# Two subtractions of the dense front move from VectorE to GpSimd, under a new merge table

## The chip, the cores and the metric

The kernel runs on one core of a Trainium2 chip. The metric is the time of one execution on the device in microseconds; lower is better. The engines of a core are TensorE (matmuls and transposes; its weight loads have a lane of their own in the profile), VectorE, ScalarE and GpSimd. Each works through its own list of instructions in order; SyncE only issues transfers here. Engines wait for each other through semaphores.

## What is computed

Two layers over x of 4 x 2048 tokens with 256 channels, all in float32. Each layer has two halves, and each half works on a layer norm of x that is scaled and shifted by rows from a conditioning vector:

```python
h = layernorm(x) * (1 + ca) + sa          # layer 0
x = x + ga * mamba(h)                     # selective scan, 512 inner channels, 16 states
h = layernorm(x) * (1 + cb) + sb
x = x + gb * dense(h)                     # router probability times one expert, gelu, 256 -> 1024 -> 256
h = layernorm(x) * (1 + ca) + sa          # layer 1
x = x + ga * delta_attn(h)                # linear scan over tokens, projection, layer norm
h = layernorm(x) * (1 + cb) + sb
x = x + gb * mixture(h)                   # gated attention-like block, then 2 relu^2 experts and a third
```

## The kernel before

The 8192 tokens are cut into 16 chunks of 512 (NCH), four to a batch row. Channels lie on the 128 partitions in two halves (KC = 2), so one tile of a chunk's 256 channels is 2 x (128 x 512).

Products that have to be exact are made from split operands: a high part (the value copied to the fp32r type) and a low part (value minus high part), multiplied as high x high, high x low, low x high (`split3`, six matmuls for 256 input channels). So each such input needs a copy on ScalarE and two subtractions, one for each half of the channels. For the dense half the input is `ff1`, its high part `f1h` and its low part `f1l`; `ff1` and `f1l` share memory.

Three streams run at once:

- the s stream, layer 0's scan, in 99 steps a chunk: mean, norm, mean, norm, turn, bc (local steps 0 to 5), dt 0 to 3 (6 to 9), gates and ct (10 to 14), z (15 to 18), softplus (19 to 22), 68 units (23 to 90), and a tail of 8 steps. In unit k VectorE does one scan of 512 tokens (line 1195) on the product `dA` that ScalarE makes into PSUM (line 1009) and on `bu` that GpSimd makes (line 909); TensorE turns the states (`hT`), and VectorE sums them into `acc` (line 1153).
- the f stream, the dense half of the chunk before: statistics (a_stats), `rstd_a`, a_norm (gives `nF`), TensorE turns it (`h1T`), ScalarE scales it to `ff1` (line 1023) and copies it to `f1h` (line 1029), the low parts, router, c0 to c7 (up products and gelu), d0 to d7 (down products), x2.
- the x stream, layer 1 of the chunk before that: norms e, h, i, j, m (`rstd_*` is a power of -0.5 that GpSimd takes, line 902; VectorE waits for it in the second half of the norm), x_bias and h_bias (GpSimd adds a row to a 128 x 1024 tile, lines 953 and 958), kq, scan, ao, lowx (`fl`), r, v, sW, and the experts o and p.

How the three are merged on each engine is written down in the table `PACE`: for every piece of the f and x streams the step of the s stream before which it is issued. Step numbers count on over chunks: 105 for chunk j is local step 6 (dt 0) of chunk j + 1, 204 is local step 6 of chunk j + 2. `weave` walks the s steps; before each it issues the pieces that are due, those of the f stream first. On an engine the order is all that the numbers set: a piece does not start at a time, it stands in a queue, behind all that was issued before it.

The pieces around the change: in the front GpSimd has its s steps mean 0, mean 1 and norm 1 (two 128 x 1024 operations, lines 921 and 922) and then none up to softplus 0. TensorE's PSUM banks go round: dt 0 takes the bank that gate 0 needs again, and it is freed by ScalarE's exponential of dt 0 (line 983). VectorE subtracts `xnl` (line 1180) before TensorE can do bc. The table places act's `h1T` and `h1h` at 105, before its dt 0.

Of the kernel before, what the change touches and what calls it, by code (L numbers as in the profile page):

```python
# [6 lines left out]
F32 = mybir.dt.float32  # L7
F32R = mybir.dt.float32r
ALU = mybir.AluOpType
# [9 lines left out]
KC = C // P  # L19
# [126 lines left out]
def since(eng, sig, chunk, k=0):  # L146

    if sig.at(chunk, k) > 0:
# [3 lines left out]

PACE = {
    "sp": {
        "mod_f": 57, "ffn_0": 83, "ffn_1": 87, "ffn_0_down": 98, "ffn_1_down": 108, "mod_x": 191, "rv": 230,
        "sw": 237, "e0_0": 238, "e0_1": 255, "e0_0_down": 258, "e0_1_down": 258, "e1_0": 266, "e1_0_down": 269,
        "e1_1": 273, "e1_1_down": 273, "out": 289,
    },
    "pool": {
        "rstd_a": 103, "rstd_e": 186, "x_bias": 186, "h_bias": 191, "rstd_h": 202, "rstd_i": 202, "rstd_j": 205,  # L160
        "rstd_m": 252,
    },
    "act": {
# [6 lines left out]
    },  # L170
    "dve": {
        "a_stats": 100, "a_norm": 104, "low0": 105, "low1": 108, "router": 110, "prob": 124, "ffn0": 152,
        "ffn1": 153, "scaled": 153, "x2": 153, "e_stats": 191, "e_norm": 191, "kq0": 198, "kq1": 198, "kq2":
        199, "kq3": 199, "beta": 199, "scan0": 201, "qs0": 202, "scan1": 202, "qs1": 202, "ao0": 203, "ao1":
        203, "h_stats": 203, "h_norm": 203, "i_stats": 204, "i_norm": 206, "j_stats": 206, "j_norm": 208,
        "lowx0": 208, "lowx1": 208, "v0": 234, "v1": 238, "att0": 245, "att1": 247, "m_stats": 248, "m_norm":
        249, "lowh0": 251, "lowh1": 251, "bids": 256, "tw0": 257, "tw1": 257, "choice": 257, "tr": 258, "e0":
        274, "e1": 291, "x5": 291,
    },
# [12 lines left out]
    },  # L192
}

# [1 line left out]
def build(nc, w, out):  # L196
    ctx = ExitStack()
    with ctx:
# [22 lines left out]
        def signal(name, n):  # L221
            return Signal(sem(name), n)
# [42 lines left out]
        f1h = sb("f1h", [P, KC, CT], F32R)  # L265
        f1l = sb("f1l", [P, KC, CT], F32R)
        ff1 = over("ff1", [P, KC, CT], "f1l")
# [46 lines left out]
        prob = sb("prob", [P, NT])  # L314
        sm = sb("sm", [P, NT, 3 * NH])
        bl = sb("bl", [P, NT, 8])
        sg = sb("sg", [P, NT, 4])
# [75 lines left out]
        f_fh = signal("f_fh", KC)  # L393
        f_fl = signal("f_fl", KC)
# [391 lines left out]
        with nc.Block() as block:  # L786
# [113 lines left out]
            def _(pool):  # L900
                def rstd(rs, sig):
                    pool.tensor_tensor(rs[:, :], rs[:, :], mhalf[:, :], ALU.pow).then_inc(sig.sem, 1)  # L902
# [35 lines left out]
                def f_stream(j):  # L938
                    yield "rstd_a"
                    pool.wait_ge(f_mv.sem, f_mv.at(j, 1))  # L940
                    rstd(rs_f, f_rs)

                def x_stream(j):
                    def norm(k):
# [166 lines left out]
            def _(dve):  # L1111
# [107 lines left out]
                def f_stream(j):  # L1219
# [7 lines left out]
                    since(dve, f_x2, j)  # L1227
                    dve.wait_ge(f_rs.sem, f_rs.at(j, 1))
                    apply(nF, x1, mv_f, rs_f, f_n)
                    for c in range(KC):  # L1230
                        yield f"low{c}"
                        dve.wait_ge(f_fh.sem, f_fh.at(j, c + 1))
                        dve.tensor_tensor(f1l[:, c, :], ff1[:, c, :], f1h[:, c, :].bitcast(F32), ALU.subtract)\
                           .then_inc(f_fl.sem, 1)
                    yield "router"
                    b = take(dve, j, "routerT")
                    dve.tensor_copy(lg[:, :, :], b.t[:, 0:NT * 8].rearrange("p (t e) -> p t e", t=NT))\
# [444 lines left out]
```

## Time and profile before

| | us |
|---|---|
| median of three runs | 3918.71 (3918.51 to 3923.24) |
| the profiled execution | 3923.29 |
| its span, first to last instruction | 3921.5 |

| engine | busy, us | share of the span | instructions |
|---|---|---|---|
| TensorE matmul | 3080.0 | 79% | 14772 |
| VectorE | 3124.9 | 80% | 5517 |
| ScalarE | 2143.5 | 55% | 3193 |
| GpSimd | 1694.7 | 43% | 1289 |

The mean granted TensorE clock is 0.878 of full speed. Busy shares are averages over stages: a front, where many short pieces wait for each other, and the units, where VectorE scans. They have to be read apart.

### The profile page before, as it was taken

The page shows a single profiled execution, that of the slowest core. Times are in us where ns is not written, and L with a number is a line of the kernel's source. Part 1 is how long each engine was busy: PE and PEld are TensorE (multiplying, and loading weights), DVE is VectorE, ACT ScalarE, POOL GpSimd, SP SyncE. Part 2 cuts the span into 40 slices and gives each one's busy share as a digit, 9 for nine tenths or more (in the row PEclk, how much of TensorE's full clock was granted, in tenths as well). Part 3 has the DMA queues.
Part 4 walks back from the last instruction along what each step waited for, and adds up shares of the span by engine and source line. Part 5 has one row for each costly group of instructions (what it writes and reads, how often), then busy time and mean ns, then how long its engine had stood idle before and what let it go on. Part 6 is the DMA issues. An engine that isn't in the chain of part 4 may idle for free. (4 is left out here: it accounts for less than half of the span.)

```text
span 3921.5 us, 44935 instructions
## 1 busy us (share of the span) xinstructions
PE 3080.0 (79%) x14772; PEld 2484.7 (63%) x14772; DVE 3124.9 (80%) x5517; ACT 2143.5 (55%) x3193; POOL 1694.7 (43%) x1289
## 2 busy tenths in 40 slices
PE   3556688797887879788787878888797978879668
PEld 1445467576675767576676757667576756757556
DVE  5777889797888879898888879798897979888331
ACT  0426375655647475564747466564747556474322
POOL 0535454453535354453545445353545445353000
PEclk7658689898998989898998989899998989989878
DMA  6110113121221312121221312122131212212111
GB/s 221 34 54 25 56 65 108 57 89 59 88 71 61 111 62 84 57 96 63 82 81 65 117 41 95 56 87 82 56 108 62 86 64 84 71 67 95 54 59 70
DMA packets 143008, 298.31 MB, mean 76 GB/s; under 512 B 18084, under 2 KB 87732, under 8 KB 125364
## 3 DMA queue, kind: packets, MB, share of 16 engines
q1 hardware_dynamic: 142232, 292.29, 22.0%
q8 instruction: 119, 1.95, 0.2%
q10 hardware_dynamic: 272, 1.57, 0.1%
q0 software_dynamic: 272, 1.57, 0.1%
q14 instruction: 113, 0.93, 0.1%
HBM read 278.04 MB, written 17.35 MB: 75 GB/s over the span
## 5 line engine op out<-in xcount | busy, mean ns | idle before, releaser
L909 POOL TENSOR_TENSOR bu<-z,bb 128x512 f32<-128x512 f32 x1024 | 1307.4, 1285 | 889.2 <-DVE hs L1195 656.1
L1195 DVE TENSOR_TENSOR_SCAN hs<-ps_A,state,bu 128x512 f32<-128x512 f32 x768 | 977.5, 1275 | 78.3 <-ACT ps_A L1009 61.8
L1009 ACT ACTIVATE ps_A<-dt,a_neg 128x512 f32<-128x512 f32 x1024 | 690.1, 686 | 514.1 <-DVE hs L1195 511.1
L1429 PE MATMUL ps_H<-ident,hs 128*128 128x128 f32 x4096 | 655.4, 299 | 308.8 <-DVE hs L1195 167.0
L1429 PEld LDWEIGHTS ps_H<-ident,hs 128*128 128x128 f32 x4096 | 526.6, 154 | 447.7 <-issue 199.2
L1153 DVE SCALAR_TENSOR_TENSOR acc<-ps_H,ctok,acc 128x512 f32<-128x512 f32 x960 | 697.2, 729 | 68.3 <-PE ps_H L1429 67.8
L1533 PE MATMUL ps_B<-ws_out,hid 128*128 128x256 f32 x3072 | 727.0, 381 | 30.8 <-ACT hid L1040 18.0
L1533 PEld LDWEIGHTS ps_B<-ws_out,hid 128*128 128x128 f32 x3072 | 565.6, 190 | 120.2 <-ACT hid L1040 24.3
L1434 PE MATMUL ps_B<-fh,ws_in 128*128 128x512 f32 x1536 | 599.2, 434 | 14.9 <-DMA ws_in<-w_split 4.8
L902 POOL TENSOR_TENSOR rs_x<-rs_x,mhalf 128x4 f32<-128x4 f32 x80 | 90.7, 1134 | 770.5 <-DVE rs_x L1120 770.5
L1434 PEld LDWEIGHTS ps_B<-fh,ws_in 128*128 128x128 f32 x1536 | 305.0, 199 | 78.8 <-DMA ws_in<-w_split 5.2
L1195 DVE TENSOR_TENSOR_SCAN hs<-ps_A,bu 128x512 f32<-128x512 f32 x256 | 310.5, 1215 | 42.5 <-ACT ps_A L1009 34.1
L1434 PE MATMUL ps_B<-f1h,ws_in 128*128 128x512 f32 x512 | 235.0, 510 | 119.1 <-ACT hid L1040 58.0
L1434 PE MATMUL ps_B<-fl,ws_in 128*128 128x512 f32 x768 | 313.5, 408 | 0.0
L1104 ACT ACTIVATE hid<-ps_B 128x512 f32<-128x512 f32 x256 | 150.5, 588 | 256.9 <-PE ps_B L1434 254.7
L1009 ACT ACT_TABLE_LOAD x191 | 245.1, 1283 | 3.4
L1434 PEld LDWEIGHTS ps_B<-f1h,ws_in 128*128 128x128 f32 x512 | 123.7, 242 | 167.5 <-ACT hid L1040 71.7
L1434 PEld LDWEIGHTS ps_B<-fl,ws_in 128*128 128x128 f32 x768 | 153.7, 200 | 22.0
L1106 ACT ACTIVATE hid<-hid 128x512 f32<-128x512 f32 x256 | 161.6, 631 | 8.2
L1405 DVE SCALAR_TENSOR_TENSOR hA<-ps_B,coef,hA 128x256 f32<-128x256 f32 x192 | 79.5, 476 | 96.1 <-PE ps_B L1533 93.8
L1273 DVE TENSOR_TENSOR fl<-ff,fh 128x512 fp32r<-128x512 f32 x64 | 67.5, 1094 | 105.9 <-ACT fh L1054 105.9
L928 POOL TENSOR_TENSOR z<-z,dt 128x512 f32<-128x512 f32 x64 | 83.8, 1310 | 136.1 <-ACT dt L996 136.1
(265 smaller groups left out, 4617.8 us busy)
## 6 DMA issues: line engine op xcount, KB each, us to landing
ws_in<-w_split SPq DMA_DIRECT2D x128, 1024.0 KB, 4.8
bb<-b_rows SPq DMA_DIRECT2D x256, 256.0 KB, 3.4
ws_out<-in_L_ffn_V_rwkv SPq DMA_DIRECT2D x64, 512.0 KB, 4.9
ws_out<-in_L_ffn_W SPq DMA_DIRECT2D x32, 512.0 KB, 5.3
w_split<-ws_in SPq DMA_DIRECT2D x8, 1024.0 KB, 4.9
xraw<-in_L_attn_x SPq DMA_DIRECT2D x16, 512.0 KB, 4.6
out<-xb SPq DMA_DIRECT2D x16, 512.0 KB, 3.3
stage<-in_L_ffn_K_rwkv SPq DMA_DIRECT2D x4, 512.0 KB, 6.7
```

The source lines that it names most:

```text
L902: pool.tensor_tensor(rs[:, :], rs[:, :], mhalf[:, :], ALU.pow).then_inc(sig.sem, 1)
L909: pool.tensor_tensor(bu[:, u % 4, :], z[:, d, :], bb[:, s % 2, :], ALU.mult).then_inc(s_bu.sem, 1)
L928: pool.tensor_tensor(z[:, k, :], z[:, k, :], dt[:, k, :], ALU.mult).then_inc(s_u.sem, 1)
L1009: act.activation(b.t[:, :], dt[:, d, :], ACT.Exp, scale=a_neg[:, d, s:s + 1])\
L1104: act.activation(hid[:, k, :], b.t[:, :], ACT.Relu).then_inc(b.free, 1)
L1106: act.activation(hid[:, k, :], hid[:, k, :], ACT.Square).then_inc(x_sq.sem, 1)
L1153: ins = dve.scalar_tensor_tensor(out=acc[:, t, :], in0=b.t[:, :], scalar=ctok[:, t, s:s + 1], in1=acc[:, t, :], op0=ALU.mult, op1=ALU.add)
L1195: dve.tensor_tensor_scan(hs[:, s % 2, d, :], b.t[:, :], bu[:, k % 4, :], state[:, s, d:d + 1] if i % CPB else 0.0, ALU.mult, ALU.add)\
L1405: ins = dve.scalar_tensor_tensor(out=hA[:, t, :], in0=b.t[:, t % 2 * C:(t % 2 + 1) * C], scalar=coef[:, t, e:e + 1], in1=hA[:, t, :], op0= ...
L1429: return pe.transpose(dst, src, ident[:, :])
L1434: last = pe.matmul(dst, a, b, start=n == 0, stop=n == len(prods) - 1)
L1533: last = pe.matmul(b.t[:, t % 2 * C:(t % 2 + 1) * C], hid[:, k, t * P:(t + 1) * P], wt[:, k % HB, :], start=k == 0 and t % 2 == 0, stop=k ...
```

## The change

GpSimd makes the low halves of the dense front's input in place of VectorE, with the same operation on the same tiles and the same semaphores. The table `PACE` is made anew for all engines: some 90 numbers move, most by one or two steps. The larger moves, and those that change an order around the front, are in the cut of the diff.

```diff
 PACE = {
     "sp": {
-        "mod_f": 57, "ffn_0": 83, "ffn_1": 87, "ffn_0_down": 98, "ffn_1_down": 108, "mod_x": 191, "rv": 230,
-        "sw": 237, "e0_0": 238, "e0_1": 255, "e0_0_down": 258, "e0_1_down": 258, "e1_0": 266, "e1_0_down": 269,
+        "mod_f": 65, "ffn_0": 90, "ffn_1": 94, "ffn_0_down": 100, "ffn_1_down": 105, "mod_x": 191, "rv": 230,
+        "sw": 242, "e0_0": 243, "e0_1": 260, "e0_0_down": 261, "e0_1_down": 264, "e1_0": 273, "e1_0_down": 273,
...
     "pool": {
-        "rstd_a": 103, "rstd_e": 186, "x_bias": 186, "h_bias": 191, "rstd_h": 202, "rstd_i": 202, "rstd_j": 205,
-        "rstd_m": 252,
+        "rstd_a": 105, "rstd_e": 196, "x_bias": 196, "h_bias": 204, "rstd_h": 215, "rstd_i": 215, "rstd_j": 215,
+        "rstd_m": 252, "low0": 107, "low1": 107,
     },
     "act": {
-        "h1T0": 105, "h1T1": 105, "h1h0": 105, "h1h1": 105, "router": 120, "lexp": 124, "c0": 126, "c1": 126,
+        "h1T0": 105, "h1T1": 105, "h1h0": 105, "h1h1": 105, "router": 120, "lexp": 124, "c0": 125, "c1": 125,
...
-        "q": 195, "kvT0": 196, "kvT1": 196, "xlT0": 218, "xlT1": 218, "xlh0": 218, "xlh1": 218, "r0": 235, "r1":
+        "q": 195, "kvT0": 196, "kvT1": 196, "xlT0": 218, "xlT1": 218, "xlh0": 220, "xlh1": 220, "r0": 235, "r1":
...
     "dve": {
-        "a_stats": 100, "a_norm": 104, "low0": 105, "low1": 108, "router": 110, "prob": 124, "ffn0": 152,
-        "ffn1": 153, "scaled": 153, "x2": 153, "e_stats": 191, "e_norm": 191, "kq0": 198, "kq1": 198, "kq2":
+        "a_stats": 102, "a_norm": 104, "low0": 105, "low1": 105, "router": 111, "prob": 124, "ffn0": 152,
+        "ffn1": 152, "scaled": 152, "x2": 152, "e_stats": 191, "e_norm": 191, "kq0": 198, "kq1": 198, "kq2":
...
-        203, "h_stats": 203, "h_norm": 203, "i_stats": 204, "i_norm": 206, "j_stats": 206, "j_norm": 208,
+        203, "h_stats": 203, "h_norm": 203, "i_stats": 205, "i_norm": 207, "j_stats": 207, "j_norm": 208,
...
     "pe": {
-        "h1T0": 105, "h1T1": 105, "router": 119, "c0": 119, "routerT": 119, "c1": 119, "c2": 120, "c3": 120,
+        "h1T0": 108, "h1T1": 108, "router": 123, "c0": 123, "routerT": 123, "c1": 123, "c2": 123, "c3": 123,
...
@@ -939,6 +939,11 @@
                     yield "rstd_a"
                     pool.wait_ge(f_mv.sem, f_mv.at(j, 1))
                     rstd(rs_f, f_rs)
+                    for c in range(KC):
+                        yield f"low{c}"
+                        pool.wait_ge(f_fh.sem, f_fh.at(j, c + 1))
+                        pool.tensor_tensor(f1l[:, c, :], ff1[:, c, :], f1h[:, c, :].bitcast(F32), ALU.subtract)\
+                            .then_inc(f_fl.sem, 1)
 
@@ -1227,11 +1232,6 @@
                     apply(nF, x1, mv_f, rs_f, f_n)
-                    for c in range(KC):
-                        yield f"low{c}"
-                        dve.wait_ge(f_fh.sem, f_fh.at(j, c + 1))
-                        dve.tensor_tensor(f1l[:, c, :], ff1[:, c, :], f1h[:, c, :].bitcast(F32), ALU.subtract)\
-                           .then_inc(f_fl.sem, 1)
```

## Rows read from the trace of the kernel before

**Rows 1.** Stretches, us: busy of PE, PEld, DVE, ACT, POOL; clock; DMA
```profile
2008.50:2083.30 74.80, 59.99 (x283) 48.54 (x282) 58.52 (x162) 34.58 (x53) 24.86 (x16) 0.87 0.15 50
2083.30:2232.40 149.10, 126.39 (x638) 103.27 (x639) 135.06 (x180) 101.12 (x148) 81.16 (x64) 0.93 0.26 89
2053.30:2075.50 22.20, 22.20 (x106) 17.70 (x104) 18.09 (x61) 14.61 (x22) 3.51 (x3) 1.00 0.15 50
2079.30:2094.20 14.90, 11.63 (x29) 8.15 (x30) 9.56 (x12) 11.67 (x17) 13.81 (x11) 0.50 0.09 32
```

**Rows 2.** Timeline (start, duration in us), TensorE, front of chunk 9
```profile
2053.31 0.58 PE L1434 MATMUL ps_H<-xnh,w_bc_h 128*128 128x512 f32 x1
...
2054.89 1.04 PE L1429 MATMUL ps_B<-ident,nF 128*128 128x128 f32 x8
...
2061.34 0.39 PE L1434 MATMUL ps_H<-w_in_h,xnh 128*128 128x512 f32 x1
...
2073.08 1.03 PE L1429 MATMUL ps_B<-ident,nn 128*128 128x128 f32 x8
...
2079.32 0.77 PE L1434 MATMUL ps_B<-f1h,ws_in 128*128 128x512 f32 x1 [3.82 <-ACT rows_f L1017]
```

**Rows 3.** Timeline, ScalarE, the same front
```profile
2055.58 1.42 ACT L1023 ACTIVATE ff<-ps_B,mod_col 128x512 f32<-128x512 f32 x2
...
2058.06 1.28 ACT L983 ACT_TABLE_LOAD   x1
2059.35 0.69 ACT L983 ACTIVATE dt<-ps_H,bdt_col 128x512 f32<-128x512 f32 x1
...
2075.73 1.43 ACT L1047 ACTIVATE ff<-ps_B,cols 128x512 f32<-128x512 f32 x2
...
2081.53 1.30 ACT L1009 ACTIVATE ps_A<-dt,a_neg 128x512 f32<-128x512 f32 x2
```

**Rows 4.** Timeline, VectorE, the same front
```profile
2051.42 1.29 DVE L1180 TENSOR_TENSOR xnl<-xnf,xnh 128x512 fp32r<-128x512 f32 x2 [2.35 <-ACT xnh L975]
...
2058.95 1.67 DVE L1135 SCALAR_TENSOR_TENSOR xb<-nn,rs_x,xb 128x256 f32<-128x256 f32 x4
...
2070.53 1.38 DVE L1124 TENSOR_SCALAR nn<-hA,mv_x,rs_x 128x256 f32<-128x256 f32 x4
2077.71 3.16 DVE L1273 TENSOR_TENSOR fl<-ff,fh 128x512 fp32r<-128x512 f32 x2 [5.80 <-ACT fh L1054]
2082.78 0.19 DVE L1237 COPY lg<-ps_B 128x32 f32<-128x32 f32 x1 [1.92 <-PE ps_B L1515]
...
2083.34 2.46 DVE L1195 TENSOR_TENSOR_SCAN hs<-ps_A,state,bu 128x512 f32<-128x512 f32 x2
```

**Rows 5.** By source line, whole run: count, ns smallest/median/largest
```profile
L1233 DVE TENSOR_TENSOR f1l<-ff,f1h x32: 681/684/693, 289.0 to 3642.2; 128x512 fp32r<-128x512 f32 x32
...
L909 POOL TENSOR_TENSOR bu<-z,bb x1024: 1258/1278/1612, 125.4 to 3577.0; 128x512 f32<-128x512 f32 x171
```

**Rows 6.** Timeline, GpSimd, front of chunk 9
```profile
2050.31 1.02 POOL L902 TENSOR_TENSOR rs_f<-rs_f,mhalf 128x4 f32<-128x4 f32 x1
2057.42 1.17 POOL L902 TENSOR_TENSOR rs_x<-rs_x,mhalf 128x4 f32<-128x4 f32 x1 [6.09 <-DVE rs_x L1120]
```

**Rows 7.** GpSimd's h_bias by line; timeline of both engines, front of chunk 1
```profile
L958 POOL TENSOR_TENSOR hA<-hA,bo_row x16: 2345/3264/3281, 462.9 to 3779.5; 128x1024 f32<-128x1024 f32 x16
...
279.44 2.34 POOL L922 TENSOR_TENSOR xb<-xraw,h 128x1024 f32<-128x1024 f32 x1
...
280.25 2.68 DVE L1180 TENSOR_TENSOR xnl<-xnf,xnh 128x512 fp32r<-128x512 f32 x2 [3.39 <-ACT xnh L975]
```

**Rows 8.** Timeline of ScalarE, TensorE and VectorE, first units of chunk 9
```profile
2086.17 0.69 ACT L1009 ACTIVATE ps_A<-dt,a_neg 128x512 f32<-128x512 f32 x1 [0.76 <-DVE hs L1195]
...
2088.91 0.79 PE L1434 MATMUL ps_B<-f1h,ws_in 128*128 128x512 f32 x1 [2.96 <-ACT hid L1040]
...
2095.03 0.75 DVE L1150 TENSOR_SCALAR acc<-ps_H,ctok 128x512 f32<-128x512 f32 x1 [2.18 <-PE ps_H L1429]
```

More of the change, by code:

```diff
@@ L154 @@
     "sp": {
-        "mod_f": 57, "ffn_0": 83, "ffn_1": 87, "ffn_0_down": 98, "ffn_1_down": 108, "mod_x": 191, "rv": 230,
-        "sw": 237, "e0_0": 238, "e0_1": 255, "e0_0_down": 258, "e0_1_down": 258, "e1_0": 266, "e1_0_down": 269,
-        "e1_1": 273, "e1_1_down": 273, "out": 289,
+        "mod_f": 65, "ffn_0": 90, "ffn_1": 94, "ffn_0_down": 100, "ffn_1_down": 105, "mod_x": 191, "rv": 230,
+        "sw": 242, "e0_0": 243, "e0_1": 260, "e0_0_down": 261, "e0_1_down": 264, "e1_0": 273, "e1_0_down": 273,
+        "e1_1": 277, "e1_1_down": 277, "out": 293,
     },
     "pool": {
-        "rstd_a": 103, "rstd_e": 186, "x_bias": 186, "h_bias": 191, "rstd_h": 202, "rstd_i": 202, "rstd_j": 205,
-        "rstd_m": 252,
+        "rstd_a": 105, "rstd_e": 196, "x_bias": 196, "h_bias": 204, "rstd_h": 215, "rstd_i": 215, "rstd_j": 215,
+        "rstd_m": 252, "low0": 107, "low1": 107,
     },
     "act": {
[1 row of a table removed]
[1 row of a table added]
         "c2": 129, "c3": 131, "c4": 133, "c5": 138, "c6": 142, "c7": 144, "h2T0": 195, "h2T1": 195, "beta": 195,
[3 rows of a table removed]
[3 rows of a table added]
         275, "p2": 280, "p3": 281, "p4": 284, "p5": 285, "p6": 288, "p7": 288,
```

20 rows, old and new, of the table PACE are left out of this document.

## Prediction

> **What bounds the kernel now.** I read the stretches first. In the middle of the run a chunk takes some 224 us: 74.8 us from the last scan of one chunk to the first scan of the next (tail, then front), and 149 us of units. In the units VectorE is busy 135 of 149 us; in the 75 us it is busy 58.5 us and TensorE 60 us, so neither alone sets them [rows 1]. What happens there is a chain, so I followed one front (chunk 9's, from 2050 us) engine by engine. All times below are of that front.
>
> TensorE issues bc at 2053.31, turns nF at 2054.89, goes through dt, gate and z without a pause and turns nn at 2073.08; the first gate product starts at 2061.34 [rows 2]. ScalarE's copies, logarithms and a table load follow z, then the first exponential for the scans at 2081.53 [rows 3]. VectorE waits 5.8 us for fh, 1.9 us for the router's transposed logits, and scans at 2083.34 [rows 4]. Its two subtractions of f1l lie between h_norm and nn, ahead of these waits, and nn is ready at 2071.9 (2070.53 + 1.38), 1.2 us before TensorE can use it. So the work that is taken off VectorE is not late for anybody. In this front the last to be waited for are TensorE up to z, and then ScalarE.
>
> **The removed work.** Two subtractions of 684 ns, 32 in all, 21.9 us [rows 5]. All of it lies in fronts, where VectorE's own waits [rows 4] swallow it: worth 0 by this chain, and at most 1.4 us a chunk, 22 us in all, if VectorE were last. Moved to GpSimd, each is taken at 1.28 us, the price of the nearest form, its 128x512 product of two SBUF tiles [rows 5]. That is 2.6 us a chunk, in a stretch where GpSimd is idle two thirds of the time [rows 1]. By itself this is harmless. Its place in GpSimd's queue and the new table are not.
>
> **GpSimd's new order.** After its two 1024-wide operations the queue was: rstd_a, then rstd_h as soon as VectorE had the variances [rows 6]. It becomes rstd_a, h_bias (191 to 204), low0 and low1 (107), and only then rstd_h, rstd_i and rstd_j (202 to 215). GpSimd goes in order, so rstd_h waits until ScalarE has made f1h; behind rstd_h stands VectorE's second half of h_norm (2058.95 [rows 4]), and behind that the x3, i and j norms, the clips of dt and nn.
>
> **TensorE's and ScalarE's new order.** TensorE turns nF not right behind bc (105) but after three dt products (108). ScalarE still takes h1T before its first dt exponential (105). So ff1, f1h, a table load and the dt exponentials all slip, and gate 0 needs the bank that the first dt exponential frees.
>
> **h_bias meets xnl.** h_bias takes 2.34 us alone, its smallest time [rows 7]. It moves from the tail to right behind rstd_a, which ends at 2051.33 [rows 6]. VectorE starts xnl at 2051.42 [rows 4]. In the front of chunk 1 the xnl pair began while GpSimd's 1024-wide addition ran (279.44 to 281.78): the pair took 2.68 us for the 1.29 us of chunk 9 [rows 4, 7]. Its first half ended some 0.55 us after GpSimd's operation, as if it had run only then. So I take: h_bias 2051.35 to 2053.7, xnl done at 2054.85 (2053.7 + 0.55 + 0.6) in place of 2052.71. TensorE is ready for bc at 2053.3, so bc starts 1.6 us late. If xnl won the race for its first half, h_bias would get in before the second half and the end would be the same within 0.2 us. The bounds are 0 (h_bias starts too late to matter) and 2.1 us.
>
> The Trainium skill, page "SBUF — State Buffer", section on the shared port pair, speaks against this place: a VectorE operation with two SBUF inputs and a GpSimd operation that reads SBUF exclude each other for a whole instruction, and whoever comes first keeps the ports. By that rule xnl waits for all of h_bias; the row of chunk 1 agrees (2.68 us for 1.29).
>
> **The sum, one front.** bc runs 2054.9 to 2056.5. A product takes 1.40 us: eight of them and the small ct, 0.5 us, lie between 2061.34 and 2073.08 [rows 2]. So three dt products end at 2060.7, the turn of nF at 2061.5, the fourth at 2062.9. ScalarE: ff and f1h, 2.5 us, from 2061.25 to 2063.75, the table load to 2065.0, the first exponential (0.69) to 2065.7 [rows 3]. Gate 0 starts at 2065.75 in place of 2061.34: a stall of 2.85 us. From there to the end of z lie 11.74 us (2073.08 − 2061.34): 2077.5, 4.4 us late.
>
> GpSimd: low0 from 2063.25 (the first f1h), low1 to 2065.8, rstd_h to 2066.9. VectorE waited for it from 2061.1 on. From its restart to the end of nn it now takes 12.95 us (2058.95 to 2071.9); one hidden subtraction less and one clip more exposed make 12.7: nn at 2079.6, 2.1 us after z. TensorE turns nn to 2080.4 and does the router to 2081.8.
>
> ScalarE: z3 at 2077.7, table load, first logarithm to 2080.2; then ff from nn 1.45 us to 2081.65, a logarithm, rows_f to 2082.8, the logarithms and fh (the table places fh two steps later), the table load, and the first exponential to 2087.0, in place of 2082.2. VectorE: fl beside GpSimd's products 84.0 to 86.6, the logits to 87.2, first scan 2087.25. That is 3.9 us later than 2083.34. Bounds: 1.2 us (no collision, TensorE's stall partly covered) and 4.8 us (the exponential's own shift).
>
> **What the units give back.** c0 and c1 move from 126 to 125 on ScalarE, ahead of the fourth exponential. Before, that exponential waited for VectorE until 2086.17 and the two gelus stood behind it; TensorE idled 2.96 us until c2 at 2088.91, then did c2, c3 at half clock and the first hT, for which VectorE waited 2.18 us until 2095.03 [rows 8]. With the gelus at once after the third exponential (85.4), c2 starts 1.4 us earlier. That wait can shrink by 1.4 us; the fourth scan still ends before. ffn0 to x2 move to 152, before the wait for fh of 0.42 us a chunk, and cover it: 0.4. The other moves in the units are of one or two steps, and SyncE's loads stay a few us ahead of their readers; I take 0, bounds ±1 us a front.
>
> **Clock.** In the front TensorE now runs at 1.00; after its 3.8 us pause ahead of c0 it runs at 0.50, the lower of its two levels [rows 1, 2]. The new pause of 2.85 us may bring the same to the gates; there each 1.40 us product would cost 1.2 to 1.4 us more, and I allow for one or two of them. The pause ahead of c0 shrinks from 3.8 to about 1 us and the one ahead of c2 to 1.5, which may give a like amount back. I take +0.3, bounds −2 and +3.4.
>
> Per front: 3.9 − 1.4 − 0.4 + 0.3 = 2.4 us. There are 14 fronts of this kind (chunks 2 to 15): 34 us. Chunk 1's front has no x stream; by the same working, without the exponential's table load, TensorE's stall is 1.9 us, less 1.4: 0.5. Chunk 0 has none. After the last chunk low0 and low1 again stand before rstd_h and cost an estimated 1.0 us (low1's and low0's places against the two subtractions saved); the statistics moved behind kq3, where VectorE waits anyway, give back an estimated 1.4. In all 34 us. The profiled run took 3923.3 us (span 3921.5), the median is 3918.7; I add the 34 to the median: **3953 us**.
>
> **Rivals.**
> 1. *The clock drops in the gates* in most fronts: some two products, 2.5 us, of which nn's lateness hides a little: 14 times about 2.2 = 31 us: 3984. For: the 3.8 us pause was followed by 0.50 [rows 1, 2]. Against: 2.85 us is shorter, and it follows ten busy microseconds. Chance 0.15.
> 2. *h_bias misses xnl and the units give back more*: 1.6 us less and the clock before c2 recovers: 0.5 to 1 us a front: 3926 to 3934. For: the two starts are 0.1 us apart. Chance 0.12, a third of it within 0.2%.
> 3. *VectorE is the bound after all* (other side, faster): if ScalarE's f1h came before VectorE's variances, rstd_h would not be held up, and the front would shrink by VectorE's 1.37 us, the units by 1.8: 15 × 3.2 = 48 us: 3871. The point of decision: low1 must end by 2057.4, when rstd_h starts now; f1h ends at 2058.06, where the table load starts [rows 3], even with the turn in its old place, and now later. Chance 0.08.
> 4. *The change moves nothing that counts*: the front's delay goes into VectorE's idle time at the start of the units (1.9 + 2.2 us). Against: these waits follow from the same chain and move with it. 3915 to 3926, chance 0.07.
>
> The forecast itself (3938 to 3970) has 0.58. Range: from rival 2's low end to just past rival 1: 3926 to 3986, leaving out 3, most of 4 and the far tail. Slower by over 0.2% (7.8 us, about what a measurement of this kernel can tell from no change): 0.58 + 0.15 + 0.08 = 0.81. Within: 0.10. Faster: 0.09.
>
> **What the new profile would show.** If right: GpSimd's rstd_h starts 2.6 us or more after f1h; VectorE's h_norm has a wait of 5 to 7 us released by GpSimd's rs_x, which it did not have; the xnl pair takes about 3.4 us in fronts from chunk 2 on; TensorE pauses 2 to 3 us at the first gate product, released by ScalarE's dt; the units get no longer. Wrong, if xnl stays at 0.69 (no collision), if h_norm doesn't wait, or if the units shrink by more than 3 us. A granted clock under 0.9 between bc and z would speak for rival 1.

## The result, and the profile after

The changed kernel takes 3985.9 us (median, 3983.87 to 3987.83) against 3919.36 us (3918.51 to 3923.24): 1.0168 times as long, interval 1.015 to 1.0185. The prediction said slower, by 34 us; it is slower by 66.5 us. The kernel before was timed again beside each group of experiments, with medians from 3920.6 to 3921.7 us; the ratios given with the experiments are against those. The profiled execution's span is 3984.6 us against 3921.5, so 63.1 of the 66.5 us can be looked for in the traces.

The page of the changed kernel, span and busy times:

```profile
span 3984.6 us, 44935 instructions
...
PE 3100.8 (78%) x14772; PEld 2501.7 (63%) x14772; DVE 3148.7 (79%) x5485; ACT 2144.0 (54%) x3193; POOL 1723.8 (43%) x1321
```

VectorE has 32 instructions fewer and yet 23.8 us more of busy time (3124.9 before): that already says that something holds instructions up while they count as busy. GpSimd has 29.1 us more. TensorE issues the same 14772 matmuls and is busy 20.8 us longer, at a mean granted clock of 0.871 against 0.878.

I then cut both traces at VectorE's scans, into fronts (last scan of a chunk to first scan of the next) and units (first to last scan of a chunk). Sums in us, worked out from the scans' start and end times:

| | prologue | units 0 | front 1 | units 1 | fronts 2 to 15 | units 2 to 15 | drain |
|---|---|---|---|---|---|---|---|
| before | 127.5 | 114.1 | 72.0 | 128.7 | 1076.9 | 2065.9 | 336.5 |
| after | 126.1 | 114.1 | 71.0 | 132.4 | 1149.2 | 2051.6 | 340.2 |
| difference | -1.4 | 0.0 | -1.0 | +3.7 | +72.3 | -14.3 | +3.7 |

A front of chunks 2 to 15 is 5.16 us longer, the units of a chunk 1.02 us shorter. The differences add up to 63.0 us.

The same stretches as in [rows 1], with the same columns, for the changed kernel: the front of chunk 9, its units, and 13.7 us of chunk 7's front, from the first gate product to the end of z:

```profile
2039.90:2119.40 79.50, 59.56 (x286) 47.50 (x285) 60.03 (x161) 34.46 (x53) 26.33 (x18) 0.91 0.14 43
2119.40:2265.90 146.50, 124.44 (x636) 103.33 (x636) 135.67 (x180) 101.19 (x148) 81.36 (x65) 0.93 0.27 93
...
1644.70:1658.40 13.70, 13.56 (x52) 10.18 (x52) 11.44 (x40) 7.42 (x13) 3.21 (x4) 0.88 0.00 1
...
1645.90:1648.90 3.00, 3.00 (x9) 2.18 (x7) 3.00 (x9) 2.38 (x3) 0.00 (x0) 0.50 0.00 0
```

The first two lines: the front grew from 74.8 to 79.5 us with the same work in it, the units went from 149.1 to 146.5. The third: from the first gate product to the end of z TensorE is busy nearly all the time (13.56 of 13.70), but the clock averages 0.88; in the kernel before it was 1.00 in this part. The fourth lies inside the third and shows the granted clock at 0.50 there. I show chunk 7 from here on because chunks 8 and 9 are the two fronts in which the clock held.

TensorE in the front of chunk 7, timeline (start, duration):

```profile
1633.84 0.50 PE L1434 MATMUL ps_H<-xnh,w_bc_h 128*128 128x512 f32 x1
...
1639.54 1.03 PE L1429 MATMUL ps_B<-ident,nF 128*128 128x128 f32 x8
...
1641.57 0.40 PE L1434 MATMUL ps_H<-xnh,w_dt_l 128*128 128x512 f32 x1
1644.72 0.50 PE L1434 MATMUL ps_H<-w_in_h,xnh 128*128 128x512 f32 x1 [2.74 <-ACT dt L988]
...
1646.20 0.63 PE L1434 MATMUL ps_H<-w_in_h,xnl 128*128 128x512 f32 x1
...
1649.94 0.40 PE L1434 MATMUL ps_A<-w_in_l,xnh 128*128 128x512 f32 x1
...
1658.44 1.09 PE L1429 MATMUL ps_B<-ident,nn 128*128 128x128 f32 x8 [0.17 <-DVE nn L1129]
```

The turn of nF now stands behind three dt products, and the first gate product waits 2.74 us for ScalarE's dt. Behind the pause the matmuls go from 0.40 to 0.63 us each and are back at 0.40 by 1649.94. nn is no longer late for TensorE: it waits 0.17 us.

ScalarE, GpSimd and VectorE in the same front, in this order:

```profile
1641.52 1.14 ACT L1034 ACTIVATE f1h<-ff 128x512 fp32r<-128x512 f32 x2
1642.68 1.28 ACT L988 ACT_TABLE_LOAD   x1
1643.98 0.69 ACT L988 ACTIVATE dt<-ps_H,bdt_col 128x512 f32<-128x512 f32 x1
...
1630.29 2.35 POOL L963 TENSOR_TENSOR hA<-hA,bo_row 128x1024 f32<-128x1024 f32 x1
1642.22 2.49 POOL L945 TENSOR_TENSOR f1l<-ff,f1h 128x512 fp32r<-128x512 f32 x2 [9.59 <-ACT f1h L1034]
1644.66 1.02 POOL L902 TENSOR_TENSOR rs_x<-rs_x,mhalf 128x4 f32<-128x4 f32 x1
...
1630.42 3.37 DVE L1185 TENSOR_TENSOR xnl<-xnf,xnh 128x512 fp32r<-128x512 f32 x2 [2.35 <-ACT xnh L980]
1645.82 1.67 DVE L1140 SCALAR_TENSOR_TENSOR xb<-nn,rs_x,xb 128x256 f32<-128x256 f32 x4 [5.83 <-POOL rs_x L902]
1657.00 1.38 DVE L1129 TENSOR_SCALAR nn<-hA,mv_x,rs_x 128x256 f32<-128x256 f32 x4 [0.90 <-POOL rs_x L902]
1664.24 2.89 DVE L1273 TENSOR_TENSOR fl<-ff,fh 128x512 fp32r<-128x512 f32 x2 [5.86 <-ACT fh L1059]
```

All four steps of the prediction are to be seen. The first dt exponential stands behind f1h and a table load and ends when the gate product starts. GpSimd idles 9.59 us for f1h, makes both low halves, and only then rs_x; h_norm waits 5.83 us for it. h_bias (L963) starts 0.13 us ahead of xnl, and the xnl pair takes 3.37 us.

By line, whole run (count, ns smallest/median/largest):

```profile
L945 POOL TENSOR_TENSOR f1l<-ff,f1h x32: 1260/1263/1477, 290.2 to 3689.1; 128x512 fp32r<-128x512 f32 x32
L963 POOL TENSOR_TENSOR hA<-hA,bo_row x16: 2340/2349/2681, 486.3 to 3842.4; 128x1024 f32<-128x1024 f32 x16
L1185 DVE TENSOR_TENSOR xnl<-xnf,xnh x32: 677/1381/2840, 96.5 to 3462.4; 128x512 fp32r<-128x512 f32 x32
```

The moved subtraction costs 1263 ns on GpSimd (684 on VectorE, [rows 5]; 1.28 us was taken). h_bias itself got cheaper (median 3264 ns before, [rows 7]): in its old place it was the one that was held up (in chunk 9 it started while VectorE's line 1215 ran and ended 2.2 us after that). Single xnl halves now reach 2840 ns for a smallest time of 677.

To say what the steps are worth on average, not in one front, I took the same marks in all fronts of chunks 2 to 15, in us after the start of xnl. The copy of z3 is ScalarE's copy of the last z product, the end of the gate and z stretch; h_norm stands for the start of its second half, nn for the start of nn:

| | end of xnl | start of bc | first gate product | copy of z3 | h_norm | nn | first scan |
|---|---|---|---|---|---|---|---|
| before | 1.29 | 2.51 | 10.55 | 22.49 | 7.70 | 19.27 | 32.53 |
| after | 3.39 | 3.44 | 14.30 | 28.03 | 15.40 | 26.59 | 37.99 |
| h1T back (e3) | | | 11.40 | 23.33 | 11.71 | 22.90 | 33.30 |
| pause filled (e9) | | | 14.31 | 26.35 | | | 36.34 |
| rstd_h first (e2) | | | | 28.05 | 9.62 | 23.89 | 38.01 |

From the first gate product to the copy of z3 lie 11.94 us before and 13.73 us after: 1.79 us more for the same products.

### The profile page after: what moved, and what is told of

The parts are those of the page before. It is cut to its first block and busy times, and to the rows that moved or that the text cites. A ratio compares the mean times of both kernels' runs of the same rounds, so it can differ in the third digit from the quotient of the medians.

```text
span 3984.6 us, 44935 instructions
## 1 busy us (share of the span) xinstructions
PE 3100.8 (78%) x14772; PEld 2501.7 (63%) x14772; DVE 3148.7 (79%) x5485; ACT 2144.0 (54%) x3193; POOL 1723.8 (43%) x1321
## 5 line engine op out<-in xcount | busy, mean ns | idle before, releaser
L1434 PE MATMUL ps_B<-f1h,ws_in 128*128 128x512 f32 x512 | 225.1, 496 | 106.5 <-ACT hid L1045 52.5
L1405 DVE SCALAR_TENSOR_TENSOR hA<-ps_B,coef,hA 128x256 f32<-128x256 f32 x192 | 79.5, 475 | 98.2 <-PE ps_B L1533 93.8
L976 ACT ACTIVATE xnf<-ps_A,cols 128x512 f32<-128x512 f32 x32 | 24.9, 777 | 236.3 <-PE ps_A L1429 235.1
L902 POOL TENSOR_TENSOR rs_s<-rs_s,mhalf 128x4 f32<-128x4 f32 x32 | 32.8, 1024 | 264.4 <-DVE rs_s L1125 264.4
```

The lines of the kernel that those rows point to most:

```text
L976: act.activation(xnf[:, c, :], b.t[:, :], ACT.Identity, scale=cols[:, c:c + 1], bias=cols[:, 2 + c:3 + c]).then_inc(b.free, 1)
L1405: ins = dve.scalar_tensor_tensor(out=hA[:, t, :], in0=b.t[:, t % 2 * C:(t % 2 + 1) * C], scalar=coef[:, t, e:e + 1], in1=hA[:, t, :], op0= ...
L1434: last = pe.matmul(dst, a, b, start=n == 0, stop=n == len(prods) - 1)
```

## The experiments

The first theory: the order of the table costs the time, above all h1T's new place, by a chain through ScalarE, and TensorE's clock adds to it. The rivals: the subtraction on GpSimd itself, GpSimd's queue (rstd_h behind the low halves), or h_bias beside xnl.

**The operation alone, and the table alone.** In e5 the kernel before gets the subtractions on GpSimd (the code as in the change) and nothing else:

```diff
-        "rstd_m": 252,
+        "rstd_m": 252, "low0": 105, "low1": 108,
```

> The kernel before with its own table, and only the two subtractions on GpSimd (low0 105, low1 108 there). The prediction's claim: the move itself is worth nothing, since VectorE's part lies ahead of waits and GpSimd is idle: 3915 to 3925. Rival (VectorE is the bound): 1.4 us a chunk less, 3898. Rival (GpSimd is late for rstd_j or the router): 3930 or more.

Measured: 3915.51 us, 0.999 (0.998 to 0.9999), a gain of 5.1 us against the median of 3920.63 in that session. In e6 the changed kernel keeps its table, number for number, and the subtractions go back to VectorE, where the table has low0 and low1 at 105:

```diff
                     rstd(rs_f, f_rs)
-                    for c in range(KC):
-                        yield f"low{c}"
-                        pool.wait_ge(f_fh.sem, f_fh.at(j, c + 1))
-                        pool.tensor_tensor(f1l[:, c, :], ff1[:, c, :], f1h[:, c, :].bitcast(F32), ALU.subtract)\
-                            .then_inc(f_fl.sem, 1)
...
                     apply(nF, x1, mv_f, rs_f, f_n)
+                    for c in range(KC):
+                        yield f"low{c}"
+                        dve.wait_ge(f_fh.sem, f_fh.at(j, c + 1))
+                        dve.tensor_tensor(f1l[:, c, :], ff1[:, c, :], f1h[:, c, :].bitcast(F32), ALU.subtract)\
+                           .then_inc(f_fl.sem, 1)
```

> The changed kernel with the subtractions back on VectorE (105, 105), the new table otherwise. Theory: the late turn of nF costs the same; GpSimd's queue is free of the low parts, which was worth nothing in the run with rstd_h first: 3980 to 3990, as the changed kernel. Rival (the move of the operation is what costs): 3950 or less.

Measured: 3985.09 us, 1.0163 (1.0147 to 1.0178); the first scan comes at 37.97 us, the changed kernel's is at 37.99. The two runs together settle it: the whole loss is in the table. The move of the work costs nothing: under the new table it is worth 0.8 us, which can't be told from 0, and under the old one it brings some 5 us (0.4 to 7.8 by the interval). In e5's trace that gain sits in four of the 14 fronts, where the first scan comes 9.08 us after the copy of z3 in place of some 10.0; the reason is given below, with e11.

**h1T back to 105.** e3 is the changed kernel with one number pair undone on TensorE:

```diff
     "pe": {
-        "h1T0": 108, "h1T1": 108, "router": 123, "c0": 123, "routerT": 123, "c1": 123, "c2": 123, "c3": 123,
+        "h1T0": 105, "h1T1": 105, "router": 123, "c0": 123, "routerT": 123, "c1": 123, "c2": 123, "c3": 123,
```

> The changed kernel with TensorE's turn of nF back at 105, ahead of the dt products. Theory 1: f1h comes 4 us earlier, TensorE has no pause ahead of the first gate product, rstd_h is held up by only 2 to 3 us; what stays is h_bias against xnl, 1.6 us, and a little of nn: 3935 to 3950, about 3940. The clock theory says the same sign and wants the granted clock back at 1.00 between bc and z. Rival (h1T's place is of no weight, GpSimd's queue is): 3975 or more.

Measured: 3914.3 us, 0.9981 (0.9971 to 0.999). That is 71.6 us less than the changed kernel, more than its whole loss, and 26 us less than the 3940 I expected. The expectation priced the pause and not the clock behind it, which e9 puts at 25 us. TensorE in the front of chunk 7:

```profile
1605.46 0.51 PE L1434 MATMUL ps_H<-xnh,w_bc_h 128*128 128x512 f32 x1 [0.91 <-DVE xnl L1185]
...
1606.96 1.04 PE L1429 MATMUL ps_B<-ident,nF 128*128 128x128 f32 x8
...
1613.42 0.40 PE L1434 MATMUL ps_H<-w_in_h,xnh 128*128 128x512 f32 x1
```

nF is turned right behind bc, the first gate product follows without a wait and at 0.40 us, and gate to z3 takes 11.93 us on average, as before (11.94). Per front the first gate product comes 2.90 us earlier, the copy of z3 4.70 us and the first scan 4.69 us. h_norm still waits for GpSimd here and h_bias still meets xnl (bc waits 0.91 us for it), so neither of these can be the main loss.

**Is it the clock?** Of the 4.7 us, the pause explains 2.9. For the other 1.8 the slower matmuls behind the pause are the suspect, but a pause and a clock that falls come together. e9 parts them: it is the changed kernel, and in the pause TensorE does the six matmuls of dt 3 twice more ahead of the real ones (the product is redone with the same result). The gate product can't start earlier by this; only the pause is filled.

```diff
                     if name == "dt":
+                        if k == DB - 1 and i >= 2:
+                            b = fill(pe, i, f"dt{k}")
+                            for _ in range(2):
+                                split3(b.t[:, :], [w_dt["h"][:, c, k * P:(k + 1) * P] for c in range(KC)],
+                                       [w_dt["l"][:, c, k * P:(k + 1) * P] for c in range(KC)],
+                                       [xnh[:, c, :] for c in range(KC)], [xnl[:, c, :] for c in range(KC)])
                         from_xn(i, f"dt{k}", w_dt, k * P)
```

> The changed kernel, with TensorE doing the fourth dt product three times over in chunks 2 to 15 (same result, 24 us... in detail 2 x 1.40 us of extra work a front), so that it works through most of its 2.85 us pause ahead of the first gate product. From gate 0 to ScalarE's copy of z3 the changed kernel takes 13.7 us on average, the kernel before 11.9. Theory (the pause lowers the granted clock): with the pause filled the stretch is 11.9 us again, 1.8 us a front, 25 us in all, against the changed kernel's 3986: about 3961, though 12 more matmuls are done in each front. Rival (the lower clock has another cause, or the work just delays): 3986 to 4010.

Measured: 3960.5 us, 1.0098 (1.0081 to 1.0115): 25.4 us less than the changed kernel, with 2.8 us of matmuls more in every front. TensorE's timeline in chunk 7, its last dt product and its first gate product:

```profile
1631.41 0.40 PE L1434 MATMUL ps_H<-xnh,w_dt_l 128*128 128x512 f32 x1
1631.76 0.50 PE L1434 MATMUL ps_H<-w_in_h,xnh 128*128 128x512 f32 x1
```

and the stretch from there to the end of z (columns as in [rows 1]):

```profile
1631.80:1643.80 12.00, 11.97 (x53) 9.17 (x52) 10.07 (x36) 7.18 (x12) 2.94 (x4) 1.00 0.01 2
```

The first gate product starts at the same place in the front (14.31 us after xnl, 14.30 without the filling), the granted clock is 1.00 where it was 0.88, and the stretch takes 12.0 in place of 13.7 us. The copy of z3 comes 1.68 us earlier, the first scan 1.65 us, and the fronts' sum is 24.9 us smaller (1.78 each). The count over all fronts agrees: with the pause of 2.74 us the granted clock fell behind it in 12 of 14 fronts in the changed kernel, in 14 in e1, 13 in e2 and 12 in e6; without it (e3) or with it filled (e9) in none. So the pause costs twice: by its own length, and by the lower clock that follows it. The filling undoes the second alone.

**GpSimd's queue.** e2 puts rstd_h ahead of the low halves again:

```diff
-        "rstd_a": 105, "rstd_e": 196, "x_bias": 196, "h_bias": 204, "rstd_h": 215, "rstd_i": 215, "rstd_j": 215,
+        "rstd_a": 105, "rstd_e": 196, "x_bias": 196, "h_bias": 204, "rstd_h": 204, "rstd_i": 215, "rstd_j": 215,
```

> The changed kernel with rstd_h at 204, ahead of low0 and low1 in GpSimd's queue; nothing else. Theory 1: VectorE's 5.8 us wait in h_norm goes, but nn was at most 2 us later than z, and in fronts at the lower clock not later at all: 0 to 2 us a front, 5 to 20 us in all, about 3975. Rival (the h_norm wait is the main cost): the 5.8 us come back in each of 14 fronts, 3905 to 3925.

Measured: 3985.48 us, 1.0161 (1.0145 to 1.0176), the same as with the queue; the 5 to 20 us that I expected did not come. The waits of the changed kernel (us in total, times, longest us):

```profile
DVE xb L1140 <- POOL rs_x L902: 81.4, 14, 5.9
...
PEld ps_H L1434 <- ACT dt L988: 46.3, 15, 3.2
```

In e2 the first of these is gone, the second is the same to the digit, and its timeline in chunk 7 has (VectorE, VectorE, TensorE):

```profile
1639.63 1.67 DVE L1140 SCALAR_TENSOR_TENSOR xb<-nn,rs_x,xb 128x256 f32<-128x256 f32 x4
...
1653.89 1.38 DVE L1129 TENSOR_SCALAR nn<-hA,mv_x,rs_x 128x256 f32<-128x256 f32 x4 [0.90 <-POOL rs_x L902]
...
1657.68 1.03 PE L1429 MATMUL ps_B<-ident,nn 128*128 128x128 f32 x8
```

h_norm waits for nothing, nn is ready at 1655.27 (1653.89 + 1.38), and TensorE takes it at 1657.68. 81.4 us of waits, the clearest new wait of VectorE in the whole trace, are worth nothing. With the clock kept (e9) nn really is late:

```profile
1645.56 1.09 PE L1429 MATMUL ps_B<-ident,nn 128*128 128x128 f32 x8 [1.79 <-DVE nn L1129]
...
1644.42 1.28 ACT L1001 ACT_TABLE_LOAD   x1
1645.71 0.63 ACT L1001 ACTIVATE dt<-dt 128x512 f32<-128x512 f32 x1
1646.25 1.45 ACT L1052 ACTIVATE ff<-ps_B,cols 128x512 f32<-128x512 f32 x2
```

TensorE waits 1.79 us, close to the 2.1 us forecast. But ScalarE, for whom the turned nn is meant, is in its table load and first logarithm until then, and takes it without a pause: the lateness hides there too. The marks say the same: from the copy of z3 to the first scan lie 9.99 us in e9 (26.35 to 36.34), and 9.96 in the changed kernel, where nn is hardly late. e9 with rstd_h first wasn't tried.

**h_bias beside xnl.** e1 puts h_bias back into the tail, in the changed kernel; e8 puts it behind rstd_a, in the kernel before. The table rows of e1, and of e8:

```diff
-        "rstd_a": 105, "rstd_e": 196, "x_bias": 196, "h_bias": 204, "rstd_h": 215, "rstd_i": 215, "rstd_j": 215,
+        "rstd_a": 105, "rstd_e": 186, "x_bias": 186, "h_bias": 191, "rstd_h": 215, "rstd_i": 215, "rstd_j": 215,
```

```diff
-        "rstd_a": 103, "rstd_e": 186, "x_bias": 186, "h_bias": 191, "rstd_h": 202, "rstd_i": 202, "rstd_j": 205,
+        "rstd_a": 103, "rstd_e": 186, "x_bias": 186, "h_bias": 204, "rstd_h": 204, "rstd_i": 204, "rstd_j": 205,
```

> The changed kernel with h_bias alone back at 191 (x_bias and rstd_e at 186). Theory 1 (three orders in the front cost the time, each by its own wait): xnl is done 2.1 us earlier, bc starts 1.6 us earlier, and the first scan with it in 14 fronts: 22 us off the changed kernel's 3986, so about 3964. Rival (the clock of TensorE, not the wait, is what costs): the pause ahead of the first gate product stays at 1.5 to 3 us and so does the time, 3980 or more.

> The kernel before with h_bias at 204 (and rstd_h, i, j right behind it): the collision with xnl alone. In the old front bc starts 2.5 us after xnl on average, and would start at 3.44: 0.9 us in 14 fronts, 13 us: about 3933. Rival (the prediction's 1.6 us a front): 3943. Rival (absorbed later in the front): 3921.

Measured: e1 3965.77 us, 1.0111 (1.0096 to 1.0126), 20.1 us less than the changed kernel. e8 3937.32 us, 1.0044 (1.0029 to 1.0059), 16.3 us more than the kernel before in that session (3921.02). xnl by line, of e1 and of e8:

```profile
L1185 DVE TENSOR_TENSOR xnl<-xnf,xnh x32: 679/688/2086, 97.3 to 3441.0; 128x512 fp32r<-128x512 f32 x32
```

```profile
L1180 DVE TENSOR_TENSOR xnl<-xnf,xnh x32: 676/1380/2834, 96.3 to 3423.4; 128x512 fp32r<-128x512 f32 x32
```

One number decides whether the median xnl half takes 688 or 1380 ns. The collision is real and costs in both kernels, but less than its 2.1 us: in e8 the first scan comes 0.78 us later (33.31 against 32.53) in each front, and the units lose 0.58 us a chunk (2074.0 against 2065.9 in all). That second part arises at one place: c2 starts 5.28 us after the first scan (5.29 before), but from there to the first hT lie 5.06 us in place of 4.55, at a mean granted clock of 0.53 in place of 0.60. So some 7 us of e8's loss stand behind slower matmuls; why the clock stays low for longer there was not tried.

**All three back.** e4 puts h1T, h_bias and the whole queue of GpSimd up to rstd_h back, and keeps the rest of the new table and the subtractions on GpSimd:

```diff
-        "rstd_a": 105, "rstd_e": 196, "x_bias": 196, "h_bias": 204, "rstd_h": 215, "rstd_i": 215, "rstd_j": 215,
+        "rstd_a": 103, "rstd_e": 186, "x_bias": 186, "h_bias": 191, "rstd_h": 202, "rstd_i": 215, "rstd_j": 215,
...
-        "h1T0": 108, "h1T1": 108, "router": 123, "c0": 123, "routerT": 123, "c1": 123, "c2": 123, "c3": 123,
+        "h1T0": 105, "h1T1": 105, "router": 123, "c0": 123, "routerT": 123, "c1": 123, "c2": 123, "c3": 123,
```

> The changed kernel with all three orders of before: h_bias 191, rstd_h 202 and h1T at 105; the subtractions stay on GpSimd and the rest of the new table stays. Theory 1: the fronts are as before and the units keep their 1 us of gain each: about 3910, 3900 to 3920. Rival (something else in the new table costs too): 3930 or more.

Measured: 3907.8 us, 0.996 (0.9946 to 0.9974). The first scan comes at 32.40 us, the kernel before has 32.53. So these three moves are the loss, and what is left of the change is a gain of some 14 us against the kernel before in that session (3921.65). Their prices alone (71.6, 20.1 and 0.4 us, from e3, e1 and e2 against the changed kernel) add up to 92; together they bring 78.1, so they overlap.

**c0 and c1 one step earlier.** e7 is the kernel before with one move of ScalarE, e10 the same with the subtractions of e5 on GpSimd:

```diff
-        "h1T0": 105, "h1T1": 105, "h1h0": 105, "h1h1": 105, "router": 120, "lexp": 124, "c0": 126, "c1": 126,
+        "h1T0": 105, "h1T1": 105, "h1h0": 105, "h1h1": 105, "router": 120, "lexp": 124, "c0": 125, "c1": 125,
```

> The kernel before with one pair of numbers changed: c0 and c1 at 125 in place of 126 on ScalarE. Theory: this alone gives the 1.0 us a chunk by which the units 2 to 15 are shorter in every kernel with the new table: 14 to 15 us off 3920, about 3905. Rival (the units' gain comes from the other moves in them): 3918 to 3922.

> The same kernel without the extra products: the move of the subtractions and c0, c1 at 125 under the old table. Both were worth 5 and 7 us alone; added up: 3905 to 3912.

Measured: e7 3913.75 us, 0.9982 (0.9973 to 0.9991), 6.9 us less than before in its session, half of what I expected and more than the rival has; e10 3908.0 us, 0.9967 (0.9957 to 0.9976), as expected. The effect on the first hT is there as forecast: from the first scan to the first acc lie 10.54 us before and 9.41 in e7, and VectorE in chunk 9 has no wait left where [rows 8] show 2.18 us:

```profile
2091.52 0.75 DVE L1150 TENSOR_SCALAR acc<-ps_H,ctok 128x512 f32<-128x512 f32 x1
```

But of these 1.13 us a chunk only 0.45 arrives in the units' sum (2059.6 against 2065.9, over 14). The rest is lost within four scans: on average the sixth scan of a chunk comes 1.13 us earlier, the eighth 0.79 and the tenth 0.48, and from there on the lead stays. In chunk 9 VectorE waits for ScalarE ahead of the eighth and the tenth scan of e7.

**More clock, to the end.** If the clock is worth 1.8 us in the gates, then it may be worth something ahead of c0, where TensorE pauses 3.8 us [rows 2] and then runs at 0.50 [rows 1]. e11 is e10 with the router's six matmuls done twice more in that pause, e12 is e4 with them done once more (redone, with the same result):

```diff
                     pe.wait_ge(f_fl.sem, f_fl.at(j, KC))
+                    b = fill(pe, j, "router")
+                    for _ in range(2):
+                        split3(b.t[:, :], [w_rt["h"][:, c, :] for c in range(KC)],
+                               [w_rt["l"][:, c, :] for c in range(KC)],
+                               [f1h[:, c, :] for c in range(KC)], [f1l[:, c, :] for c in range(KC)])
                     from_f(j, "router", w_rt["h"], w_rt["l"], 0, f1h, f1l)
```

> The kernel before with the two subtractions on GpSimd and c0, c1 at 125, and TensorE doing the router product three times (same result), 2.8 us of extra work a chunk inside its 3.8 us pause ahead of c0. Clock theory: c0 to c3 then run at the full clock, the router's logits and the first hT come 1 to 3 us earlier in each chunk, against the same kernel without the extra products (about 3910): 3870 to 3895. Rival (the extra work delays ScalarE's rows_f, or the clock does not follow the pause): 3905 to 3930.

> The changed kernel with the three orders of before, and the router product done twice (1.4 us in a pause of 2.8 us ahead of c0). Clock theory: the remaining pause of 1.4 us keeps the full clock, and 1 to 2.5 us a chunk come off 3908: 3870 to 3895. Rival: 3900 to 3925.

Measured: e11 3904.43 us, 0.9964 (0.9953 to 0.9975), e12 3907.41 us, 0.9969 (0.9955 to 0.9982). Neither differs from its kernel without the filling (3908.0 and 3907.8) by more than the intervals, and both miss what I expected (3870 to 3895). TensorE's timeline of e11, the starts of c0 and c2 of chunk 9:

```profile
2064.67 0.47 PE L1434 MATMUL ps_B<-f1h,ws_in 128*128 128x512 f32 x1 [0.83 <-ACT rows_f L1022]
...
2071.83 0.50 PE L1434 MATMUL ps_B<-f1h,ws_in 128*128 128x512 f32 x1 [3.24 <-ACT hid L1045]
```

and the stretch of c0 (columns as in [rows 1]):

```profile
2064.60:2067.00 2.40, 2.04 (x11) 1.44 (x11) 2.24 (x4) 2.37 (x4) 2.32 (x2) 1.00 0.00 0
```

The filling worked: the wait ahead of c0 is 0.83 us in place of 3.82, and the clock behind it is 1.00, in all 14 fronts of e11 and of e12. What it is worth depends on who waits for c0's end. TensorE makes the router's transposed logits behind c0, and VectorE copies them (`lg`) before its first scan. VectorE's copy in chunk 9, in e10 and in e11:

```profile
2072.02 0.19 DVE L1237 COPY lg<-ps_B 128x32 f32<-128x32 f32 x1 [1.64 <-PE ps_B L1515]
```

```profile
2066.68 0.19 DVE L1237 COPY lg<-ps_B 128x32 f32<-128x32 f32 x1
```

Under the old table the logits are last. From the copy of z3 to the first scan lie some 10.0 us in the kernel before and in the eight fronts of e10 where c0 runs at 0.50, but 9.08 in the six fronts of e10 where the clock held, and 9.05 to 9.22 in all of e11. That is 0.55 us a front from e10 to e11 (9.64 to 9.09 on average). The profiled runs give most of it back elsewhere: bc starts 0.34 us later after xnl, for which I know no reason, and the drain is 3.0 us longer. Under the new table the logits are not last: from z3 to the first scan lie 9.93 to 9.98 us in 13 of 14 fronts of e4 and of e12, whatever the clock at c0. And c2 starts no earlier: in e11 it now waits 3.24 us for ScalarE's gelu (1.63 in e10). TensorE ended its products earlier and stood still for longer. My expectation was wrong in taking the whole clock gain for a time gain.

This also places e5's gain. In its trace the fronts are 3.9 us shorter in all, and the four short ones are the four in which the clock at c0 was 0.81 to 1.00; in the other ten it was 0.50. Why it held in those four is not shown.

## Why the prediction was right, and what it had wrong

The measured 3985.9 lies at the very edge of the range (3926 to 3986), in the class with 0.81 of the chance, and at the time of rival 1 rather than at that of the forecast. That it lies inside by 0.1 us is luck. So is part of the agreement with rival 1 (3984): its mechanism is the one that e9 shows, but it was priced at 31 us more than the forecast, where the clock accounts for 20.7, and the difference is made up by terms that have nothing to do with it.

- **VectorE's work removed, worth 0; GpSimd's new work harmless:** right for the changed kernel, by e6. Under the old table the move brings some 5 us (e5), inside the bound of 22. The prediction names ScalarE's exponential as the last to be waited for in the old front; its own rows have VectorE waiting 1.92 us for the logits after it, and e5, e10 and e11 show that this wait counted. GpSimd's subtraction is 1.26 us where 1.28 was taken.
- **GpSimd's queue:** the wait is there as described (5.83 us in chunk 7, 5 to 7 forecast), and with the clock kept nn is 1.79 us behind z (2.1 forecast). It is worth nothing (e2), because TensorE in most fronts is no longer ahead of nn, and ScalarE has other work in the meantime.
- **h1T at 108, the pause:** right. 2.74 us in chunk 7 against 2.85; first gate product at 14.30 us on average, 14.33 in the prediction's sum (2065.75 − 2051.42).
- **h_bias meets xnl:** the pair takes 3.39 us against 3.43. What it costs was too high: bc starts 0.93 us later (3.44 against 2.51), not 1.6. The prediction took chunk 9, where bc started 1.88 us after xnl; over the fronts this is 1.8 to 3.4. One front was taken for the mean.
- **First scan 3.9 us later:** without the clock's part it is 3.81 (36.34 in e9 against 32.53). Right.
- **The clock, +0.3 with bounds −2 and +3.4:** this is the step that failed. It is 1.78 us a front, 24.9 us in all (e9). The rival was described properly, "some two products", but its chance of 0.15 rested on the pause being shorter than the 3.8 us one and following ten busy microseconds. Neither helped: in 12 of 14 fronts the clock fell. What kept it up in the other two is not shown.
- **The units give back 1.8 us a chunk:** 1.02. The first acc comes 1.27 us earlier (9.27 against 10.54), near the 1.4 forecast, but by e7 less than half of such a gain stays in the units. A wait that shrinks at the start of a long stretch was counted whole. The 0.4 for ffn0 to x2 was not tried alone.
- **The rest, about 0:** +5.0 us by the table of stretches, of which units 1 and the drain have 3.7 each. In the drain VectorE now waits for TensorE's ffn0 product where it was issued earlier:

```profile
3758.09 0.69 DVE L1251 TENSOR_TENSOR nn<-ps_B,b_row 128x512 f32<-128x512 f32 x1 [4.17 <-PE ps_B L1533]
```

  This is read from the trace, not tried. The units of chunk 1 are as long in e1, e2, e3, e4 and e12 (132.0 to 132.5 us) and not in e7 and e10 (128.4), so their 3.7 us come from the rest of the new table; from which move stays open.

So the sum of 34 us lacks 32.5: 20.7 for the clock (1.48 more in 14 fronts), 10.9 for the units (0.78 in 14 chunks), some 5 for the rest, less 7.3 because the fronts without the clock, scan to scan, grew by 3.38 and not by 3.9 (5.16 − 1.78), and 3.4 us by which the medians differ more than the profiled spans. That makes 32.7.

The other rivals: VectorE isn't the bound (e6, where it does its work again, is no slower). That h_bias misses xnl happened in no front: even in chunk 14, where xnl began first:

```profile
3232.59 3.45 DVE L1185 TENSOR_TENSOR xnl<-xnf,xnh 128x512 fp32r<-128x512 f32 x2 [2.35 <-ACT xnh L980]
3232.81 2.68 POOL L963 TENSOR_TENSOR hA<-hA,bo_row 128x1024 f32<-128x1024 f32 x1
```

The first half took its usual 693 ns and the second, behind h_bias, 2837 ns; the pair ended where the prediction put it for this order too.

## What to carry to other kernels

Price a new pause of TensorE twice: its own length, and the same products at the lower clock behind it, wherever those products are on the chain (here a pause of 2.74 us brought 1.8 us more). Do not count a clock gain, or a wait that vanishes, before you have looked who is last there: in e12 and e2 it was another engine, and the gain was 0; in e11 it was the logits, and only part of the gain arrived.

When a piece is moved by a few steps in an in-order queue, ask first which bank or tile its reader frees. Here the transposes of nF stood behind three products instead of ahead of them, and undoing that alone won 71.6 us, while the moved work of the title cost nothing. And take the size of a wait from all fronts, not from the one that was followed.

## What the hardware showed that I had not expected

A pause of 2.74 us, behind 8 us in which TensorE had worked almost without a gap, was followed by the lower of its two clock levels (1.2 in place of 2.4 GHz) in 12 of 14 fronts and not in the other two; I can't say what parts the two kinds. Matmuls went from 0.40 to 0.63 us in the modelled rows, gate to z3 from 11.94 to 13.73 us, and redundant matmuls in the pause made the kernel 25.4 us faster.

VectorE's subtraction and GpSimd's addition hardly overlap, in either order. With h_bias first (13 of 14 fronts) the pair's first half ends 0.55 us after it, where it takes 0.69 us alone. With xnl first (one front, chunk 14) h_bias (2.35 us alone) gets in between the two halves, although these are issued back to back, and takes 2.68 us. The Trainium skill, page "SBUF — State Buffer", section on the two separate sides, has the lock for a whole instruction, whoever starts first; the traces agree (2837 ns for a half of 693 beside a GpSimd operation of 2.68 us).
